# Gated layers of an fp32 kernel: the rank 2 parts of gate and up projection as two products of 32 rows on row quarters 0 and 1

## What is computed

```python
def _qlora_linear(x, wq, A, B):
    w = jnp.tile(wq, (1, 4))
    base = x @ w.T
    lora = x @ A.T @ B.T
    return base + lora * LORA_SCALING          # 0.5
gate = jax.nn.silu(_qlora_linear(x, w1q, a1, b1))
up = _qlora_linear(x, w3q, a3, b3)
return _qlora_linear(gate * up, w2q, a2, b2)
```

## Time and profile before

| | us |
|---|---|
| median of 3 runs | 2243.18 (2241.72 to 2245.71) |
| the profiled execution | 2240.26 |
| its span, first to last instruction | 2238.6 |
| TensorE busy / DVE / POOL / ACT | 2070.0 / 1435.0 / 1000.0 / 919.3 |
| stage B on TensorE | about 345 to 821 us of the span |

### The profile page before, as it was taken

How to read it: one execution, slowest core, us unless ns; L and a number is a source line. 1 busy time by engine, 2 the same in 40 slices (tenths; PEclk the granted TensorE clock), 3 DMA queues, 4 the chain that set the end, 5 groups by cost and what they waited for, 6 DMA issues and landing times.

```text
span 2238.6 us, 30651 instructions
## 1 busy us (share of the span) xinstructions
PE 2070.0 (92%) x10504; PEld 1468.4 (66%) x10504; DVE 1435.0 (64%) x3291; ACT 919.3 (41%) x1891; POOL 1000.0 (45%) x866
## 2 busy tenths in 40 slices
PE   5788977999999989989999999899998999999998
PEld 4545436888888879755556556465543787676687
DVE  8986789666667663477675776577679555444333
ACT  5755664223333333145554555455556232221111
POOL 1344677444444420038765677578763231210000
PEclk9999998999999999999999999999988999999999
DMA  5211275122222157412224632222223673343332
GB/s 181 94 81 51 93 237 204 38 76 76 76 76 76 66 188 262 105 41 61 78 66 126 176 81 72 75 76 60 67 73 105 209 239 132 132 174 109 113 114 93
DMA packets 139595, 249.25 MB, mean 111 GB/s; under 512 B 26910, under 2 KB 69790, under 8 KB 139216
## 3 DMA queue, kind: packets, MB, share of 16 engines
q1 hardware_dynamic: 128432, 227.37, 32.0%
q10 hardware_dynamic: 11008, 19.93, 2.8%
HBM read 139.48 MB, written 76.02 MB: 96 GB/s over the span
## 4 chain that ended last, share of the span: by engine, by line
PE 59%; POOL 13%; DVE 9%; issue 3%; ACT 2%; DMA 1%; SPq 1%; ACTq 1%; POOLq 0%; DVEq 0%
POOL c_S L2405 8%; PE PS L2574 5%; PE PS L2578 5%; PE PS L2575 5%; PE PS L2617 5%; PE PS L1113 3%; PE PS L1114 3%; PE PS L1115 3%; PE PS L1973 3%; PE PS L1988 3%; PE PS L1955 3%; PE PS L1146 2%; PE PS L1147 2%; PE PS L1148 2%; DVE PS L2297 2%
## 5 line engine op out<-in xcount | busy, mean ns | idle before, releaser
L2142 ACT ACTIVATE c_P<-PS 128x512 f32<-128x512 f32 (+3 forms) x768 | 357.6, 494 | 322.8 <-PE PS L1973 304.0
L1955 PE MATMUL PS<-c_K,c_Q 96*128 96x512 f32 (+3 forms) x768 | 278.0, 372 | 23.2 <-DVE cst L2297 14.6
L1973 PE MATMUL PS<-c_Q,c_K 97*128 97x512 f32 (+3 forms) x768 | 282.3, 381 | 7.8 <-DMA c_Q<-c_mT 5.0
L2405 POOL TENSOR_TENSOR c_S<-c_S,c_P 128x2048 f32<-128x2048 f32 (+3 forms) x94 | 272.5, 2899 | 8.5
L1973 PEld LDWEIGHTS PS<-c_Q,c_K 97*128 97x128 f32 x768 | 147.6, 194 | 175.5 <-ACT c_P L2142 97.9
L2293 DVE TENSOR_REDUCE cst<-PS 128x1 f32<-128x512 f32 x256 | 176.0, 687 | 90.9 <-PE PS L1955 90.2
L1955 PEld LDWEIGHTS PS<-c_K,c_Q 96*128 96x128 f32 x768 | 151.0, 197 | 79.7 <-DVE cst L2297 38.7
L1988 PE MATMUL PS<-c_P,c_V 128*32 128x512 f32 (+3 forms) x1536 | 168.7, 512 | 14.1 <-ACT c_P L2142 9.6
L2297 DVE CUSTOM_DVE_ANT_0 PS<-PS,maskw,cst 128x128 f32<-128x128 f32 (+3 forms) x256 | 142.9, 558 | 59.6 <-PE PS L1955 43.4
L199 POOL TENSOR_TENSOR maskw<-maskw,mhalf 128x1 f32<-128x1 f32 x64 | 38.0, 593 | 317.5 <-DVE maskw L168 317.2
L2297 DVE CUSTOM_DVE_ANT_0 PS<-PS,maskw 128x128 f32<-128x128 f32 (+3 forms) x256 | 126.5, 504 | 65.4 <-PE PS L1955 63.3
(11 more groups left out here) (291 smaller groups left out, 4862.4 us busy)
## 6 DMA issues: line engine op xcount, KB each, us to landing
a_xin<-in_x SPq DMA_DIRECT2D x32, 512.0 KB, 4.2
d_x<-scr SPq DMA_DIRECT2D x32, 512.0 KB, 4.4
c_Q<-c_qh SPq DMA_DIRECT2D x240, 64.0 KB, 2.0
scr<-a_xin SPq DMA_DIRECT2D x16, 512.0 KB, 6.2
b_xn<-scr SPq DMA_DIRECT2D x16, 512.0 KB, 5.5
b_x<-scr SPq DMA_DIRECT2D x16, 512.0 KB, 4.7
scr<-b_x SPq DMA_DIRECT2D x16, 512.0 KB, 2.6
scr<-b_y SPq DMA_DIRECT2D x16, 512.0 KB, 3.0
```

Of the source, the lines that this page charges most:

```text
L1955: e.matmul(bank[:, 0:hi - lo], self.Q4[0:96, 4 * (o % 3) + g, 128 * t:128 * t + 128], self.K4[0:96, HEADS[o % 8], lo:hi], start=True, stop ...
L1973: e.matmul(self.k.bank(i % 3)[:, 0:hi - lo], self.K4[0:97, HEADS[o % 8], 128 * kt:128 * kt + 128], self.Q4[0:97, 4 * (o % 3) + g, lo:hi], ...
L2142: e.activation(self.P[:, R % 3, g, 0:hi - lo], self.k.bank(i % 3)[:, 0:hi - lo], ACT.Exp, scale=SCALE).then_inc(self.exp_s.s, 1)
L2405: e.tensor_tensor(S[:, :, 512 - n:512], S[:, :, 512 - n:512], P[:, :, 0:n], ADD).then_inc(self.psum_s.s, 1)
```

## The change

`ux` and `bx` have 64 rows in place of 96. Gate has rows 0 to 31 and up rows 32 to 63. In each quarter stand the three products of its own v in rows 2q and 2q + 1: high, low, high of B against high, high, low of u. The last product of gate and that of up are issued one behind the other, after all twelve products of 128 rows of the chunk, each on its quarter of the array's rows. `pe_low` is one product with 64 results. The splits are made by a mask column in `cst`, 1 in the rows that want the low part and 0 in those that want the high part, with signs in `sel` that suit. The waits for `lowd_s` and `blo_s` stand before the pair; the wait for `up_s` of the tile before moves from ScalarE to VectorE. Two spare tensors (`gap0`, `gap1`) take the memory that comes free. In `lay_out`, on the host, `bx`, `sel` and two columns of `cst` are written to match.

```diff
-            self.bx = sb("bx", [96, FH], F32R)
-            self.a13, self.sel = sb("a13", [128, 8, 32]), sb("sel", [128, 2, 96])
+            self.bx = sb("bx", [64, FH], F32R)
+            self.a13, self.sel = sb("a13", [128, 8, 32]), sb("sel", [128, 64])
+            sb("gap0", [128, 128])
...
     def pe_low(self, e, t):
         e.wait_ge(*self.usb_s(t + 1))
         o = self.k.bank(5)
-        for v in range(2):
-            m = e.matmul(o[0:96, 128 * v:128 * v + 128], self.sel[:, v, :], self.usb[:, :], start=True, stop=True)
-        m.then_inc(self.low_s.s, 1)
+        e.matmul(o[0:64, 0:128], self.sel[:, :], self.usb[:, :], start=True, stop=True).then_inc(self.low_s.s, 1)
...
-            if c == 0 and v == 0:
-                e.wait_ge(*self.lowd_s(t + 1))
-            if t == 0 and c % 2 == 0 and v == 0:
-                e.wait_ge(*self.blo_s(c // 2 + 1))
-            m = e.matmul(o, self.ux[:, par, v, :], self.bx[:, C0[c]:C0[c] + n], start=False, stop=True)
+        if c == 0:
+            e.wait_ge(*self.lowd_s(t + 1))
+        if t == 0 and c % 2 == 0:
+            e.wait_ge(*self.blo_s(c // 2 + 1))
+        for v in range(2):
+            rows = slice(32 * v, 32 * v + 32)
+            m = e.matmul(k.bank(2 * (p % 2) + v)[:, 0:n], self.ux[rows, par, :], self.bx[rows, C0[c]:C0[c] + n], start=False,
+                         stop=True)
         m.then_inc(self.up_s.s, 1)
...
-        o = self.k.bank(5)[:, 0:256].rearrange("p (v n) -> p v n", v=2)
-        e.copy(self.ux[0:64, t % 2, :, :], o[0:64])
-        e.copy(self.ur[64:96, :, :], o[64:96]).then_inc(self.lowc_s.s, 1)
+        e.copy(self.ur[:, :], self.k.bank(5)[0:64, 0:128]).then_inc(self.lowc_s.s, 1)
...
-        e.tensor_tensor(self.bx[32:64, cols], self.bx_in[32:64, cols], self.bx[32:64, cols].bitcast(F32), SUB
-                        ).then_inc(self.blo_s.s, 1)
+        e.scalar_tensor_tensor(out=self.bx[:, cols], in0=self.bx_in[:, cols], scalar=self.k.cst[0:64, 386:387],
+                               in1=self.bx[:, cols].bitcast(F32), op0=MUL, op1=SUB).then_inc(self.blo_s.s, 1)
...
-        e.tensor_tensor(self.ux[64:96, t % 2, :, :], o[64:96], self.ur[64:96, :, :].bitcast(F32), SUB).then_inc(self.lowd_s.s, 1)
+        if t >= 2:
+            e.wait_ge(*self.up_s(6 * (t - 1)))
+        e.scalar_tensor_tensor(out=self.ux[:, t % 2, :], in0=self.k.bank(5)[0:64, 0:128], scalar=self.k.cst[0:64, 385:386],
+                               in1=self.ur[:, :].bitcast(F32), op0=MUL, op1=SUB).then_inc(self.lowd_s.s, 1)
```

More of the change, by code:

```diff
@@ L993, in __init__ @@
             self.usb = sb("usb", [128, 128])
-            self.ux, self.ur = sb("ux", [96, 2, 2, 128], F32R), sb("ur", [96, 2, 128], F32R)
+            self.ux, self.ur = sb("ux", [64, 2, 128], F32R), sb("ur", [64, 128], F32R)
+            sb("gap1", [128, 384])
             self.g = [sb(f"g{i}", [128, 460]) for i in range(3)]
             self.prod = [sb("pr0", [128, 460])]
-            with nc.sbuf_tensor("b_bx_in", [96, FH], F32) as bx_in:
+            with nc.sbuf_tensor("b_bx_in", [64, FH], F32) as bx_in:
                 self.bx_in = bx_in
@@ L1032, in sp_a13 @@
         e.dma_start(self.a13[:, :, :], io["a13T"].rearrange("(c p) n -> p c n", p=128)).then_inc(self.ldw.s, 16)
-        e.dma_start(self.sel[:, :, :], io["sel"]).then_inc(self.ldw.s, 16)
+        e.dma_start(self.sel[:, :], io["sel"]).then_inc(self.ldw.s, 16)
     def sp_a2(self, e):
@@ L1233, in act_low @@
             e.wait_ge(*self.lowd_s(t))
-        if t >= 2:
-            e.wait_ge(*self.up_s(6 * (t - 1)))
-        o = self.k.bank(5)[:, 0:256].rearrange("p (v n) -> p v n", v=2)
-        e.copy(self.ux[0:64, t % 2, :, :], o[0:64])
-        e.copy(self.ur[64:96, :, :], o[64:96]).then_inc(self.lowc_s.s, 1)
+        e.copy(self.ur[:, :], self.k.bank(5)[0:64, 0:128]).then_inc(self.lowc_s.s, 1)
     def act_silu(self, e, t, c):
@@ L2853, in lay_out @@
     cst[:, 384] = 1.0 / 128
+    for v in range(2):
+        cst[32 * v + 4:32 * v + 6, 385] = 1.0
+        cst[32 * v + 2:32 * v + 4, 386] = 1.0
     cst[:, 392:520] = np.where(np.arange(128)[None, :] > np.arange(128)[:, None], -1.0e38, 0.0)
@@ L2867, in lay_out @@
     d["w13"] = np.concatenate([w13[..., C0[c]:C0[c] + NS[c]].reshape(128, -1) for c in range(6)], 1)
-    bx = np.zeros((96, FH), f)
+    bx = np.zeros((64, FH), f)
     for q in range(3):
-        bx[32 * q:32 * q + 2] = g["L0_ffn_b1"][hid].T
-        bx[32 * q + 2:32 * q + 4] = g["L0_ffn_b3"][hid].T
+        bx[2 * q:2 * q + 2] = g["L0_ffn_b1"][hid].T
+        bx[32 + 2 * q:32 + 2 * q + 2] = g["L0_ffn_b3"][hid].T
     d["bx"] = bx
@@ L2879, in lay_out @@
     d["w2x"] = np.concatenate([g["L0_ffn_w2q"].T, g["L0_ffn_b2"].T])
-    sel = np.zeros((128, 2, 96), f)
+    sel = np.zeros((128, 64), f)
     for c in range(4):
[L2882 to L2885, removed]
+        for v in range(2):
+            for q in range(3):
+                for r in range(2):
+                    sel[32 * c + 2 * v + r, 32 * v + 2 * q + r] = -0.5 if q else 0.5
     d["sel"] = sel
```

## The result

| | before | changed |
|---|---|---|
| median, 5 runs each, us | 2241.72 (2240.96 to 2245.71) | 2252.76 (2248.74 to 2255.27) |
| the profiled execution | 2240.26 | 2252.76 |
| its span | 2238.6 | 2251.1 |

The changed kernel is slower: ratio 1.0037, 95% interval 1.0024 to 1.0050, that is 8.3 us with 5.4 to 11.2 us as its bounds. The medians differ by 11.0 us. With two more runs the median of the kernel before is 2241.72 us; of the three runs ahead of the prediction it was 2243.18.

A forecast was written before the change was run, and what follows sets the result against it. TensorE's order, about 400 to 800 us, bounds the kernel. 58 x 0.20 = 11.6 plus 14 x 0.07 = 1.0 makes 12.6 us on 2240.3, 2252.9; the median stands 2.9 higher: 2255.8 us. Range 2248 to 2274, at 0.80.

The forecast's parts named there:

- What bounds: Stage B, about 400 to 800 us: TensorE's order is the path; a chunk's added cost reaches the end one for one.
- The step in: Entering row quarters after a chunk's last L1115: 0.30 us until the pair's first weights are loaded.
- The four records of L2606: fp32 products on one row quarter, weights loaded 0.32 us after the last whole product; evidence that row quarters pause too.
- Second quarter, 0.01: Within a pair: the second quarter follows the first by 0.01 us, as it is another quarter.
- rival B: Slower still: quarters change form but don't run side by side; 2264.3 us, or 2272.8 if products stream in turn; chance 0.20.
- The way out: Behind the pair: 0.30 us until the next product may load, taken from a span of 0.20 to 0.30.
- The uncovered load, 0.11: At the pair and at the next product: a weight load no longer hidden, 0.11 us each time.
- Pairs ahead of the fold: Chunk 3, tiles 2 to 14: 0.72 us before and now, so no difference, 13 x 0.
- `pe_low`, the one small cost: Behind chunk 4 of tiles 1 to 14: 1.39 us against 1.32, +0.07 each, 1.0 us in all.
- Tile 0 and `dve_blo`: Tile 0's pairs hidden by waits, else up to 1.2 us; `dve_blo` in stage A's tail 1.11 us, at most 1.2 us extra.
- A: Rival, faster: entering and leaving a row quarter costs nothing, weights load ahead as before; 2227.2 us, chance 0.16.
- C: Rival: forms change nothing and the pair runs in turn; +1.0 us, 2244.2 us, chance 0.04.

The follow-up runs named there:

- e2_apart: Changed kernel with each quarter product at the end of its own v, so the two stand apart; 2309.72 us, ratio to before 1.0294.
- e5_fold: e4_four with transposes moved behind chunks 0 and 1 and the fold right behind chunk 2's four products; 2227.01 us, ratio to before 0.9935.
- e7_same: Changed kernel with both products of a pair on row quarter 0; 2276.78 us, ratio to before 1.0159.
- e4_four: Changed kernel with four products on four row quarters behind chunks 0, 2 and 4, low step on the whole array; 2229.07 us, ratio to before 0.9949.
- e3_low96: Changed kernel with 96 columns in the selecting matrix instead of 64, 32 of them zeros; 2250.59 us, ratio to before 1.0036.

## Why the prediction was right

**Direction and size.** Forecast was +12.6 us and 2255.8 us, measured +11.0 by the medians, 5.4 to 11.2 by the ratio's interval, and 2252.76 us, inside the range of 2248 to 2274. The forecast is above the interval's upper end, so its sum was somewhat too large. Of the 3.0 us between 2255.8 and 2252.76, 1.5 is the median of the kernel before, which the forecast started from at 2243.18, and 1.6 the change itself.

**What bounds.** TensorE's order from 400 to 800 us, one for one: every tile is longer by the same 0.69 us, and nobody else waits for a new reason. Shown by e2_apart to e5_fold, where a saving or a cost on that order comes out in the tile to 0.14 us at most.

**The step in.** 0.30 forecast, 0.29 to 0.31 in all kernels. The four records of L2606 were a sound witness that quarters of the rows behave like quarters of the columns.

**Second quarter, 0.01.** Right, and rival B wrong with it: the loads of a pair last 0.18 us together, as one alone. e7_same shows what B had priced at +0.20: both products on one quarter cost 0.21 us more. The 4 ns of the Trainium skill ("TensorE: Matmul & The Clock Gate", Part 3) agree with the trace: four records in e4_four last 0.01 us longer than two. By that trace their four starts lie 3 to 4 ns apart.

**The way out.** 0.11 + 0.01 + 0.30 = 0.42 forecast from the pair's load to the next, 0.40 measured ahead of whole-array work. The difference is small, but it counts at every pair.

**The uncovered load, 0.11.** With the way out, the term that was mis-sized. I took it for every follower from one of 512 columns. It holds where products of 460 columns follow (e2_apart). Where transposes follow it is less, and they follow three pairs in a tile. From the last L1115 of a chunk to that of the next, the two traces differ as follows (us, medians of 11 tiles, rounded; a negative number is time gained):

| chunk | 0 | 1 | 2 | 3 | 4 | 5 | tile |
|---|---|---|---|---|---|---|---|
| follows the pair | transposes | transposes | transposes | fold | `pe_low` | next tile's chunk 0 | |
| forecast | 0.20 | 0.20 | 0.20 | 0 | 0.07 | 0.20 | 0.87 |
| measured | 0.15 | 0.14 | 0.15 | -0.03 | 0.12 | 0.17 | 0.69 |

So the whole-array followers cost 0.14 to 0.17 in place of 0.20. About 0.02 of each miss is the way out; most of what is left is the load. Taken as the extra distance between the first two products behind the pair, it was 0.09, 0.05 and 0.09 us at chunks 0 to 2, where transposes follow, and 0.10 at chunk 5.

**What was said to cost nothing.** Pairs ahead of the fold: 0.30 + 0.40 = 0.70 now, 0.72 before, as said. `pe_low`, the one small cost: +0.07 forecast, as 1.39 us from the last L1115 to the second product of the third projection against 1.32; measured 578.97 - 577.56 = 1.41. Nearly right. Tile 0 and `dve_blo`: the changed kernel is 2.4 us later by tile 1's low step, of which 1.3 are there long ahead of any edit. `dve_blo` took 1.30 us on the mean in place of 1.11, 1.16 in two of its three instructions and 1.58 in the last, below its bound of 1.71:

```profile
L1325 DVE SCALAR_TENSOR_TENSOR b_bx<-b_bx_in,cst,b_bx 64x920 fp32r<-64x920 f32 (+1 forms) x3 | 3.9, 1301 | 0.0
```

What of the rest belongs to the edits in stage A's tail stays open. That the profiled execution's +12.5 us meets the forecast's +12.6 is luck: the steady tiles are 2.3 us below the forecast (13 x 0.18), and the start, in good part scatter, is about as much above.

**The rivals.** A (no price for the form) would have shown the pair's weights loaded as those of any whole-array product are, while the product before still streams; they wait 0.31 us 83 times. The sign that I had written down for A, weights that load ahead of L1115's end, was badly chosen: L1115's record ends at 577.56 + 0.37 = 577.93 and the pair loads at 577.86, and the fold of the kernel before does the same (563.97 against 563.67 + 0.37). What tells the two apart is the 0.30 us from start to load, and the tile. C would have had records of two products one behind the other, as e7_same does.

## What to carry to other kernels

Packing two small products side by side saves one of them, and the change of form around them costs its own amount once, here 0.37 us for 0.21 saved; so count the products per change of form, not the idle rows. With four in one group the same technique gained 13 us (interval 7 to 16; about 0.1 of the 0.94 us per tile is that the low step is one product in place of two), and with the group next to a step that changes form anyway 0.17 us more per tile. Padding a small product to the whole array can be cheaper than its own form (e3_low96), and placing an accumulation's small term first in one bank and last in another is a way to bring such products together.

## What the runs showed of the hardware beyond the prediction

- The price of a change of form did not depend on the form. Behind products of 460 columns, quarters of the rows, quarters of the columns and halves of the rows all took 0.30 us in. The way out, load to load, was 0.40 for row quarters and row halves of 460 columns. From row quarters straight to column quarters was one change of 0.42, not two.
- Wider can be cheaper: the low step with 96 results in place of 64, zeros included, shortened the tile by 0.18 us, as expected once the forecast's terms were known.
